# Three more stage buffers, E2's copies between the weights' copies, and 11 row groups on ScalarE in the start-up of a transformer layer

## What is computed

```python
x = x + attention(layernorm(x))   # Wqkv 1024 x 768, one head of 256, softmax over 2048, Wo 256 x 1024
y = layernorm(x)                  # without gamma and beta
h = relu(y @ up_w) ** 2           # 1024 x 2048
shared = h @ down_w               # 2048 x 1024
latent = (y @ fc1_w) @ expert_w   # 1024 x 512, 512 x 512
moved = (latent * sum(top2(y @ gate_w))) @ fc2_w
x = x + layernorm(shared + moved) * gamma + beta
```

## Time and profile before

| | before |
|---|---|
| median of 3 runs | 2407.22 us |
| profiled execution | 2406.86 us |
| its span | 2404.8 us |
| TensorE busy | 2317.7 us, 96% |
| VectorE busy | 1742.0 us, 72% |
| GpSimd busy | 1566.4 us, 65% |
| ScalarE busy | 907.1 us, 38% |
| mean granted clock of TensorE | 0.987 of full |

### The profile page before, as it was taken

The page is one execution under the profiler, slowest core; times in us unless marked ns, Lnnn a source line. Parts: engine busy times, 40 slices in busy tenths (PEclk is TensorE's granted clock), DMA queues, the critical chain, the costliest instruction groups (busy, mean ns, idle before and its releaser), DMA issues.

```text
span 2404.8 us, 31321 instructions
## 1 busy us (share of the span) xinstructions
PE 2317.7 (96%) x11224; PEld 1935.1 (80%) x11224; DVE 1742.0 (72%) x2946; ACT 907.1 (38%) x1707; POOL 1566.4 (65%) x1180
## 2 busy tenths in 40 slices
PE   7999999999998999999999999999999999999996
PEld 5888889888887788878778887787888788788875
DVE  5889857877877454854689764479795368977869
ACT  4222233333332353443433443442354343244442
POOL 4456535664665676598658479847649975844584
PEclk8999999999999999999999999999999999999998
DMA  8899847778777643535336343535434543633452
GB/s 232 265 308 303 250 134 198 213 227 299 199 213 212 199 114 94 126 92 149 101 119 185 96 127 92 149 96 164 140 112 112 133 112 108 186 107 98 120 154 91
DMA packets 218970, 386.48 MB, mean 161 GB/s; under 512 B 19648, under 2 KB 99648, under 8 KB 218176
## 3 DMA queue, kind: packets, MB, share of 16 engines
q1 hardware_dynamic: 217664, 382.38, 55.2%
q10 hardware_dynamic: 1152, 2.10, 0.2%
HBM read 260.67 MB, written 90.18 MB: 146 GB/s over the span
## 4 chain that ended last, share of the span: by engine, by line
PE 56%; DVE 19%; POOL 10%; DMA 7%; issue 4%; SPq 3%; ACT 1%; DVEq 0%; POOLq 0%; ACTq 0%
PE ps L2154 19%; PE ps L2156 18%; PE ps L2155 18%; DVE pturn L1334 5%; DMA pland<-pturn 4%; POOL hq L2000 3%; POOL wr1l L1918 2%; SPq L640 2%; POOL wr2l L1918 2%; POOL wr0l L1918 2%; DVE x L1361 2%; DVE mx L1319 2%; DMA stf<-downs 1%; DVE xi L1272 1%; DVE st L1364 1%
## 5 line engine op out<-in xcount | busy, mean ns | idle before, releaser
L1918 POOL TENSOR_TENSOR wr1l<-stf,wr1h 128x512 fp32r<-128x512 f32 x183 | 260.1, 1421 | 155.7 <-ACT wr1h L965 155.7
L1918 POOL TENSOR_TENSOR wr0l<-stf,wr0h 128x512 fp32r<-128x512 f32 x184 | 261.3, 1420 | 147.1 <-ACT wr0h L965 146.9
L1918 POOL TENSOR_TENSOR wr2l<-stf,wr2h 128x512 fp32r<-128x512 f32 x183 | 258.6, 1413 | 149.8 <-ACT wr2h L965 149.7
L965 ACT CAST wr1h<-stf 128x512 fp32r<-128x512 f32 x183 | 113.9, 623 | 315.6 <-PE ps L2156 255.4
L965 ACT CAST wr2h<-stf 128x512 fp32r<-128x512 f32 x183 | 113.9, 622 | 304.1 <-PE ps L2156 252.2
L965 ACT CAST wr0h<-stf 128x512 fp32r<-128x512 f32 x184 | 114.5, 622 | 292.9 <-PE ps L2156 247.3
L1918 POOL TENSOR_TENSOR pt<-pland,pt 128x512 fp32r<-128x512 f32 x120 | 153.3, 1312 | 65.4 <-ACT pt L943 65.2
L930 ACT ACTIVATE prob<-ps,nm 128x512 f32<-128x512 f32 x128 | 86.2, 686 | 250.6 <-DVE nm L1327 250.6
L1334 DVE STREAM_TRANSPOSE pturn<-prob 128x512 f32<-128x512 f32 x128 | 131.7, 1092 | 63.7 <-DMA pland<-pturn 61.1
L1214 DVE TENSOR_TENSOR hr2l<-hq,hr2h 128x512 fp32r<-128x512 f32 x78 | 94.6, 1213 | 89.7 <-ACT hr2h L988 89.7
L1214 DVE TENSOR_TENSOR hr0l<-hq,hr0h 128x512 fp32r<-128x512 f32 x78 | 94.2, 1208 | 88.1 <-ACT hr0h L988 88.0
(11 more groups left out here) (488 smaller groups left out, 7765.5 us busy)
## 6 DMA issues: line engine op xcount, KB each, us to landing
stf<-ups SPq DMA_DIRECT2D x160, 256.0 KB, 3.2
stf<-downs SPq DMA_DIRECT2D x160, 256.0 KB, 3.2
stf<-in_upw_dram SPq DMA_DIRECT2D x120, 256.0 KB, 2.7
pland<-pturn SPq DMA_DIRECT2D x112, 256.0 KB, 4.7
stf<-in_down_dram SPq DMA_DIRECT2D x88, 256.0 KB, 2.8
x<-in_x_dram SPq DMA_DIRECT2D x32, 512.0 KB, 6.8
x1d<-x SPq DMA_DIRECT2D x32, 512.0 KB, 5.5
xi<-in_x_dram SPq DMA_DIRECT2D x28, 512.0 KB, 9.8
```

Of the source, the lines that this page charges most:

```text
L965: eng.copy(hi, src).then_inc(*a_w.up(K))
L1918: eng.tensor_tensor(lo, src, hi.bitcast(F32), ALU.subtract).then_inc(*done)
```

## The change

It adds stage buffers 5, 6 and 7 at places that are free during the start-up, and a table `STG_BUF` that gives each piece its buffer in place of `index % 5`. The slabs (1, 0), (2, 0) and (1, 1) have the new buffers to themselves and are loaded with no wait; (2, 1), (0, 0) and (0, 1) take the buffers of et(2), f2(2, 0) and f2(2, 1).

Low parts: et(2) and f2(2, 0) go from VectorE to GpSimd, ahead of GpSimd's wait for the root; et(3) goes from GpSimd to VectorE, behind `nb1`; f2(2, 1) stays on VectorE, but stands ahead of the mean's difference.

ScalarE's order: the high part of slab (1, 0) is made ahead of the wait for `nb1`. ScalarE scales 11 groups of the first chunk in place of 12, VectorE 5 in place of 4. E2's copies out of PSUM of row tiles 0 and 1 stand behind slab 0's and slab 1's high parts, ahead of the high parts of (1, 1) and (2, 1).

```diff
--- before.py
+++ after.py
@@ -168,7 +168,7 @@
         XI = [sb("xi0", [128, 16, 256], 192), sb("xi1", [128, 16, 256], 172)]
         XT = [sb("xt0", [128, 512], 208), sb("xt1", [128, 512], 210), sb("xt2", [128, 512], 168),
               sb("xt3", [128, 512], 170)]
-        stageA = [sb(f"sta{i}", [128, 1024], kb) for i, kb in enumerate((128, 132, 212, 136, 140))]
+        stageA = [sb(f"sta{i}", [128, 1024], kb) for i, kb in enumerate((128, 132, 212, 136, 140, 160, 164, 188))]
         pb = [sb(f"pb{i}", [128, 4, 256], kb) for i, kb in enumerate((128, 132, 136, 140, 188))]
 
         pt = [[sb(f"pt{b}{p}", [128, 16, 256], 64 + 32 * b + 16 * p, F32R) for p in range(2)] for b in range(2)]
@@ -228,9 +228,10 @@
         STG = [("et", 0), ("f2", 0, 0), ("f2", 0, 1), ("et", 1), ("f2", 1, 0), ("f2", 1, 1), ("et", 2),
                ("f2", 2, 0), ("f2", 2, 1), ("f2", 3), ("et", 3), ("w", 1, 0), ("w", 2, 0), ("w", 1, 1),
                ("w", 2, 1), ("w", 0, 0), ("w", 0, 1)]
-        STG_DVE = [("et", 0), ("f2", 0, 0), ("f2", 0, 1), ("f2", 1, 1), ("et", 2), ("f2", 2, 0), ("f2", 2, 1)]
+        STG_BUF = [0, 1, 2, 3, 4, 0, 1, 2, 3, 4, 0, 5, 6, 7, 1, 2, 3]
+        STG_DVE = [("et", 0), ("f2", 0, 0), ("f2", 0, 1), ("f2", 1, 1), ("f2", 2, 1), ("et", 3)]
         SLAB_DVE = [(0, 0), (0, 1), (0, 2)] + [(c, 0) for c in range(1, 8)]
-        NORM_DVE = (3, 7, 11, 15)
+        NORM_DVE = (3, 6, 9, 12, 15)
         SLABS = [(c, j) for c in range(8) for j in range(8)]
         PREP = prep_steps()
         PT_DVE = [(0, 1), (0, 3), (1, 0), (1, 2), (15, 0), (15, 2), (31, 0), (31, 2)]
@@ -380,7 +381,7 @@
         d_cst = dma("d_cst", [0], 2)
         d_xh = dma("d_xh", [0], 4)
         d_xi = [dma(f"d_xi{i}", [c for c in range(8) if c % 2 == i], 4) for i in range(2)]
-        d_st = [dma(f"d_st{i}", STG[i::5]) for i in range(5)]
+        d_st = [dma(f"d_st{i}", [k for k, b in zip(STG, STG_BUF) if b == i]) for i in range(8)]
         d_e2 = dma("d_e2", range(4), 2)
         d_pb = [dma(f"d_pb{b}", [k for i in range(b, 40, 5) for k in ([(i, 0), (i, 1)] if i >= 20 else [(i, 1)])])
                 for b in range(5)]
@@ -512,7 +513,7 @@
 
 
         def stg_parts(k):
-            t = stageA[STG.index(k) % 5]
+            t = stageA[STG_BUF[STG.index(k)]]
             if k[0] == "et":
                 return eth[:, k[1], :], etl[:, k[1], :], t[:, 0:512]
             if k[0] == "f2":
@@ -575,12 +576,13 @@
 
             def load_stage(k):
                 i = STG.index(k)
-                if i >= 5:
-                    w.wait_ge(*stg_lo(STG[i - 5]))
+                b = STG_BUF[i]
+                if b in STG_BUF[:i]:
+                    w.wait_ge(*stg_lo(STG[max(j for j in range(i) if STG_BUF[j] == b)]))
                 src = {"et": lambda a: expt[a // 2, :, 512 * (a % 2):512 * (a % 2) + 512],
                        "f2": lambda a, h=None: fc2[a] if h is None else fc2[a, :, 512 * h:512 * h + 512],
                        "w": lambda part, half: wqkv[2 * part + half]}[k[0]](*k[1:])
-                eng.dma_start(stageA[i % 5][:, 0:src.shape[-1]], src).then_inc(*d_st[i % 5].up(k))
+                eng.dma_start(stageA[b][:, 0:src.shape[-1]], src).then_inc(*d_st[b].up(k))
 
             def prep_load(i):
                 b, (c, half) = i % 5, divmod(i, 2)
@@ -898,7 +900,7 @@
 
             def stage_hi(k):
                 hi, _, src = stg_parts(k)
-                w.wait_ge(*d_st[STG.index(k) % 5][k])
+                w.wait_ge(*d_st[STG_BUF[STG.index(k)]][k])
                 eng.copy(hi, src).then_inc(*a_stg.up(k))
 
             def e2_evac(lt):
@@ -1011,7 +1013,7 @@
                 eng.activation(h, h, ACT.Square).then_inc(*a_act.up((n, q, c)))
 
 
-            for k in STG[:11]:
+            for k in STG[:12]:
                 stage_hi(k)
             w.wait_ge(*v_nb[0])
             for g in range(16):
@@ -1019,14 +1021,13 @@
                     xg = XI[0][:, g, :]
                     ins = eng.activation(xg, xg, ACT.Identity, bias=nb1[:, g:g + 1], scale=rst1[:, g:g + 1])
             ins.then_inc(*a_norm.up(0))
-            for k in STG[11:13]:
-                stage_hi(k)
-            for j in range(2):
-                slab_hi(0, j)
+            stage_hi(STG[12])
+            slab_hi(0, 0)
+            e2_evac(0)
+            slab_hi(0, 1)
+            e2_evac(1)
             for k in STG[13:15]:
                 stage_hi(k)
-            for lt in range(2):
-                e2_evac(lt)
             for c in range(8):
                 for j in range(8):
                     if j == 0:
@@ -1623,12 +1624,12 @@
             low(stg_parts(("f2", 1, 1)), a_stg["f2", 1, 1], v_stg.up(("f2", 1, 1)))
             aggr1(0, stats1(0, 0, 8), 0, 8)
             aggr1(0, stats1(0, 8, 16), 8, 16)
+            low(stg_parts(("f2", 2, 1)), a_stg["f2", 2, 1], v_stg.up(("f2", 2, 1)))
             diff1(0)
-            for k in STG_DVE[4:]:
-                low(stg_parts(k), a_stg[k], v_stg.up(k))
             rstd1(0)
             w.wait_ge(*v_rst[0])
             eng.tensor_tensor(nb1[:, :], nmean1[:, :], rst1[:, :], ALU.mult).then_inc(*v_nb.up(0))
+            low(stg_parts(("et", 3)), a_stg["et", 3], v_stg.up(("et", 3)))
             norm1(0, NORM_DVE)
             for j in range(2):
                 turn1(0, j)
@@ -2008,10 +2009,10 @@
                 ins.then_inc(*g_xb.up((n, t)))
 
 
-            for k in (("et", 1), ("f2", 1, 0)):
+            for k in (("et", 1), ("f2", 1, 0), ("et", 2), ("f2", 2, 0)):
                 stage_low(k)
             w.wait_ge(*v_rst[0])
-            for k in (("f2", 3), ("et", 3), ("w", 1, 0)):
+            for k in (("f2", 3), ("w", 1, 0)):
                 stage_low(k)
             for k in (("w", 2, 0), ("w", 1, 1), ("w", 2, 1)):
                 stage_low(k)
```

## The result

The changed kernel took 2402.23 us (median of 20 runs, 2398.33 to 2408.90), the kernel before, run beside it, 2407.06 us (20 runs, 2401.00 to 2412.36). The ratio is 0.9977, 95% interval 0.9969 to 0.9986: faster by 0.23%, about 5.5 us by the ratio and 4.8 by the medians. Forecast were 2402.9 and a gain of 4.3.

What follows compares the result with a forecast made beforehand. TensorE's pace was taken as the bound, with gains from its pauses or low clock. 2.65 + 1.7 = 4.35, taken as 4.3 us, off 2406.86 gives 2402.6; the median's 0.36 makes 2402.9, range 2399.5 to 2408.

Steps and rivals of the forecast that it cites:

- The bank wait: After E2, TensorE no longer waits for a PSUM copy: first projection matmul at 40.4 instead of 43.05, 2.65 us.
- The clock drop: In the projection after E2: without the 2.02 us pause no fall to the 1.2 GHz level, 1.7 us.
- E2's restart: Start-up: E2's second half restarts on TensorE at 26.0 instead of 26.82, and E2 ends 0.6 us earlier.
- the lower bound: E2 on TensorE: the clock's rise stays at 30.4 despite the earlier restart, so E2 ends only 0.4 us earlier.
- Held by GpSimd: Start-up low parts: GpSimd's running instruction fully blocks VectorE's on the shared SBUF port; f2(2,1) ends at 24.7.
- Buffers and groups: Stage buffers 5 to 7 and groups 11 and 5: loads land in time, slab 0 keeps 2.0 us of slack.
- What is late next: Projection: GpSimd's low parts of slabs 2 and 3 become the thin place, with slack 1.2 and 0.3 us.
- The carry: From V at 62.7 to the end: fixed hand-over order passes the shift on; scaling 8.1 us, fourth V tile waits 2.4.
- The rival "more": Second chunk: prep falls behind VectorE's scaling, or the pause at 78 gets too short for a drop; gain 6 to 8, chance 0.2.

Runs made afterwards that it cites:

- e2_only: The kernel before, with only E2's copies of row tiles 0 and 1 moved behind slab 0's and slab 1's high parts: 2406.62 us, ratio 0.9991.
- e2_back: The changed kernel with E2's copies moved back behind the high parts of (1,1) and (2,1): 2405.51 us, ratio 0.9988 against the kernel before.
- pause2: e2_back with TensorE also made to wait for E2's fourth copy ahead of its first projection matmul: 2407.84 us, ratio 0.9995 against the kernel before.
- five_bufs: The changed kernel with five stage buffers used in turn, as before: 2404.68 us, ratio 0.9992 against the kernel before.
- twelve: The changed kernel with 12 groups of the first rows on ScalarE and 4 on VectorE, as before: 2404.18 us, ratio 0.9982 against the kernel before.
- prep_late: The changed kernel with GpSimd's first prep instruction waiting until VectorE has scaled the second chunk: 2399.41 us (7 runs), ratio 0.9961 against the kernel before.
- prep_late2: prep_late's kernel run once more, beside the changed kernel on the same chip: 2399.67 us (12 runs), ratio 0.9964 against the kernel before.

## Why the prediction was right

The forecast was a gain of 4.3 us, and the ratio says 5.5 with an interval of 3.4 to 7.5; V's start, read from the statistics, says 4.3, 4.8 and 5.0 in three traces. That the time came within 0.7 us of 2402.9 is in part luck: two more sets of 12 runs of the same kernel gave 1.2 us (with no change inside the interval) and 4.6 by their ratios. The mechanism stands on the traces. The terms, one by one:

- *The bank wait.* Right in kind: E2's copies were what the first projection matmul waited for, although the timeline of before names VectorE's low part. e2_only shows it. In size 43.05 to 39.90, 3.15 us, for 2.65; 0.55 of it is that the rows landed earlier in this trace, which leaves 2.6.
- *The clock drop.* 1.7 us, and 1.7 it was (23.98 to 22.28 us from projection to V) in the first trace; in the other two slab 3's lateness takes 0.3 and 0.5 of it back. That a drop goes with such a pause is what the sum took from one row; e2_back and pause2 agree, but over all traces 10 of 33 pauses of 2 us and more had none. What the sum needed was only that no pause means no drop, and from 38 us to V no trace without a pause has one.
- *E2's restart.* Forecast 26.0, measured 25.02: the rows came 0.55 earlier, the variance step 0.2 earlier still, and TensorE goes on 0.2 us ahead of it (25.22), where I took one moment for both. f2(2,1) took 1.10 us, held, for the forecast 1.16. The clock came back at 30.4 as before, so of 1.8 us only 0.97 reached E2's end. This was the lower bound's mechanism. In other traces it came back sooner, so the moment is not tied to the restart. This is the term that was sized too small: 0.8 us at the restart and 0.6 at E2's end, where the traces give 1.2 and, on average, 1.3.
- *Held by GpSimd.* f2(2,1) started at 22.92, GpSimd's instruction ended at 23.47, and it ended at 24.02, 0.55 later: held, then run at its own pace. At half speed up to 23.47 and full speed behind it, it would have ended at 23.9, too near to tell. et(3) tells: it started at 27.82 and ended at 30.70, 0.55 behind GpSimd's f2(3) (30.15), where at half speed it would have ended near 29.2. The prediction took the rule that the later of the two fully blocks from the Trainium skill, SBUF — State Buffer, section "SBUF: two separate sides"; et(3) agrees with it.
- *Buffers and groups.* Forecast at nothing; five_bufs and twelve show nothing up to V.
- *What is late next.* GpSimd's slab 3, with 0.3 us of slack: it became a wait of 0.2 us in two of the traces, and cost up to 0.5.
- *The carry.* The scaling took 8.1 us again and the fourth V tile waited 2.5 again in all three traces of the changed kernel, and at wo they stand 4.7, 4.7 and 5.6 us ahead of before. That the lead passes on by a fixed order holds less than it was said: in five_bufs and e2_back, with a wait of 2.96 us in the eighth chunk, 3.8 and 3.4 us of it were gone at wo. The rival "more" was real, only not reached by this change: in e2_only, where prep came 4.5 us into the scaling, V to the second chunk was 2.2 us shorter, and in prep_late 3.2.

What the prediction left out is the size of chance: it allowed for clock drops at later pauses, but the spread between executions behind the start-up (9 us in two traces of one kernel) is larger than the change, and a median of 12 runs can hide it altogether.

## What to carry to other kernels

Where a wait names one engine, look whether the thing named had long been done; here a PSUM bank's copy, queued in ScalarE's order behind two weight copies, was the real holder, and moving that copy gave about three quarters of the gain. Of a pause, count also the clock behind it, as a chance and not as a certainty. Follow a lead past the place where it was made: here a wait seven chunks later could take it back. And look for prep work on GpSimd that runs beside a chain of VectorE instructions on SBUF: delaying it into GpSimd's idle time gave 3 us for one wait.

## What the runs showed of the hardware

- After E2, a pause of TensorE of 1.17 us left the granted clock at 2.4 GHz; pauses of 2.02 and 3.40 us were followed by a stretch at 1.2 GHz that cost 1.7 and 1.55 us. Over the first 350 us of thirteen traces, behind E2, no pause of 0.7 to 1.8 us (45 of them) had a fall of the clock in it or within 3 us behind it, and 23 of 33 pauses of 2.0 to 3.4 us had.
- 16 scaling instructions of VectorE on 128x256 in SBUF took 5.26 us alone and 8.1 us beside six GpSimd instructions of 0.7 to 0.9 us, which take 0.74 to 0.80 us behind the scaling (prep_late2): VectorE lost by it, GpSimd hardly. VectorE's statistics and transposes beside GpSimd's low parts were not slower (0.34 and 0.7 us each in both cases).
- The second half of the first rows was ready at 18.8 to 20.3 us. Within one load order the spread is as large: 18.81 to 20.16 in three kernels with that of before, 18.90 to 20.20 in the nine traces with eight buffers. It bounds the start.
